# Second self-attention: both head parities in one item, and later keys zeroed after the exponential instead of masked before it

## The reference, cut to what matters

```python
x_norm = x * rsqrt(mean(x*x) + 1e-5) * w_norm
qkv = bit_linear(x_norm, w_qkv)          # 32 query heads, 8 key/value heads, 8 wide
q, k = apply_rotary(q, cos, sin), apply_rotary(k, cos, sin)
scores = einsum('bkgsd,bktd->bkgst', q, k) / sqrt(8)
scores = where(tril, scores, -inf)
attn = softmax(scores, axis=-1)          # 256 queries by 256 keys, causal
out = einsum('bkgst,bktd->bkgsd', attn, v)
return bit_linear(out, w_out)
```

## Time and profile before

| | us |
|---|---|
| median of 3 runs | 3753.85 (3726.41 to 3762.97) |
| the profiled execution's own time | 3760.45 |
| span of the profiled execution | 3758.7 |
| busy over the span: PE, DVE, ACT, POOL | 3073.0, 1924.6, 1550.5, 1177.8 |
| first memset of the stage's token part (POOL) | starts at 2034.49 |
| last DVE instruction of the stage | starts at 2724.14, lasts 0.88 |

### The profile page before, as it was taken

How to read it: one execution, slowest core, us unless ns; L and a number is a source line. 1 busy time by engine, 2 the same in 40 slices (tenths; PEclk the granted TensorE clock), 3 DMA queues, 4 the chain that set the end, 5 groups by cost and what they waited for, 6 DMA issues and landing times. The chain is left out here.

```text
span 3758.7 us, 50944 instructions
## 1 busy us (share of the span) xinstructions
PE 3073.0 (82%) x13981; PEld 1795.9 (48%) x13983; DVE 1924.6 (51%) x4543; ACT 1550.5 (41%) x3160; POOL 1177.8 (31%) x1058
## 2 busy tenths in 40 slices
PE   5799999879999768788794799999957742888884
PEld 2477777557777534444353333333234411355553
DVE  5666666756666567777614455554232340223323
ACT  3555555545555347777511233332225410023331
POOL 1477777367777400000001000000010027044443
PEclk8899999989999855555597589887759965699997
DMA  1122121021111073000000000000000024077885
GB/s 57 46 53 52 35 50 19 12 79 35 51 51 35 23 231 107 1 1 0 27 0 16 0 1 1 1 0 0 1 20 1 0 85 145 9 161 163 182 178 122
DMA packets 127085, 192.73 MB, mean 51 GB/s; under 512 B 17552, under 2 KB 88208, under 8 KB 125584
## 3 DMA queue, kind: packets, MB, share of 16 engines
q1 hardware_dynamic: 83696, 134.71, 12.7%
q0 software_dynamic: 23616, 33.24, 5.0%
q10 hardware_dynamic: 19584, 22.57, 2.2%
HBM read 123.23 MB, written 67.25 MB: 51 GB/s over the span
## 5 line engine op out<-in xcount | busy, mean ns | idle before, releaser
L228 DVE SCALAR_TENSOR_TENSOR h_pre<-h_px,h_par,h_pre 128x510 f32<-128x510 f32 (+2 forms) x384 | 286.5, 746 | 271.3 <-ACT h_pre L689 251.4
L843 POOL TENSOR_TENSOR norm_rstd<-norm_mv,mhalf 128x4 f32<-128x4 f32 x24 | 28.2, 1177 | 1134.9 <-DVE norm_mv L826 1134.9
L652 PE MATMUL h_po<-h_wo,h_h 128*128 128x256 f32 x1024 | 329.9, 413 | 0.0
L2921 POOL DMA_INDIRECT moe_sums<-ex_y,ex_sidx x132 | 204.8, 1552 | 321.0 <-DVE ex_y L3089 304.1
L574 POOL TENSOR_SCALAR h_decay<-h_cumb,h_sel 128x256 f32<-128x256 f32 x256 | 291.6, 1139 | 25.3 <-DMA h_cumb<-cum_rows 25.3
L585 POOL TENSOR_TENSOR h_mix<-h_decay,cb 128x768 f32<-128x768 f32 x128 | 232.9, 1819 | 167.1 <-ACT h_decay L675 167.1
L616 PE MATMUL h_px<-x_cols,h_w 128*128 128x512 f32 x512 | 254.4, 620 | 25.4 <-DMA h_d<-d_skip 25.4
L2038 DVE TENSOR_REDUCE at_nmax<-at_pd 128x2 f32<-128x512 f32 (+1 forms) x192 | 132.5, 690 | 258.9 <-PE at_pd L1772 256.7
L621 PE MATMUL h_pz<-x_cols,h_w 128*128 128x512 f32 x512 | 241.7, 594 | 6.3 <-DVE h_gate L742 6.3
L1256 ACT ACTIVATE xq_ex<-xq_ps,xq_nmax,xq_qs 128x512 f32<-128x512 f32 x256 | 199.4, 779 | 113.6 <-DVE xq_nmax L1324 113.2
L1921 ACT ACTIVATE at_ex<-at_ps 128x512 f32<-128x512 f32 x192 | 114.5, 597 | 291.3 <-PE at_ps L1798 159.7
(11 more groups left out here) (397 smaller groups left out, 6498.6 us busy)
## 6 DMA issues: line engine op xcount, KB each, us to landing
h_cumb<-cum_rows SPq DMA_DIRECT2D x32, 1024.0 KB, 8.4
moe_tiles<-blank SPq DMA_DIRECT2D x4, 6642.0 KB, 44.1
ex_w<-moe_w SPq DMA_DIRECT2D x64, 352.0 KB
ex_xg<-moe_tiles ACTq DMA_DIRECT2D x136, 162.0 KB
ex_wd<-moe_wd SPq DMA_DIRECT2D x64, 176.0 KB
h_w<-w_xg SPq DMA_DIRECT2D x8, 1024.0 KB, 10.4
moe_sums<-blank SPq DMA_DIRECT2D x2, 2176.0 KB, 26.7
h_wo<-w_out SPq DMA_DIRECT2D x8, 512.0 KB, 10.3
```

The source lines that it names most:

```text
L228: ins = dve.scalar_tensor_tensor(out=out[:, :, back:S], in0=src[:, :, 0:S - back], scalar=par[:, at + CK - 1 - back:at + CK - back], in1=o ...
L652: pe.matmul(po[t // TPB][:, t % TPB, :], hh[j % 2][:, t * P:(t + 1) * P], w_out[s.pg][:, j, :], start=(j == 0 and t % TPB == 0), stop=(j = ...
L2921: pool.indirect_dma_start(out=r.sums[i % 2][:, :], out_offset=bass.IndirectOffsetOnAxis(ap=sidx[i][:, 0:1], axis=0), in_=y[i % 2][:], in_o ...
```

## The change

- **Items.** An item is now both head parities: 12 items per batch instead of 24. `at_pd` and `at_ps` become one tile of two banks each (one parity per bank), so `top` reduces 1,024 columns and `exp` takes 1,024.
- **Order of matmuls.** `score` issues even and odd head alternately (partitions 0 to 47, then 64 to 111), then one mask matmul per bank (L1774) for all its heads. `tscore` does the same with 64 rows.
- **Mask.** `tscore` has no mask matmul. Instead POOL sets the exponentials of later keys to zero in place (`select`, L1709, two per item) and `mix` waits for that (`cut`).
- **Mix.** `mix` runs once per group: four matmuls of 512 columns into four strips of 32 partitions, then four of 256. `at_po` is one bank instead of two, and ACT makes the copy (`mcopy`).
- **Elsewhere.** The values are written by ACT (`value`), `splits` and `maxsplit` take both token tiles at once, `qturn` is four pieces in four slots, key and value tiles have three buffers, and two small DVE scalings fold into others.
- **Order of slots.** Every step has a place counted from the batch's first slot (`due`), with 24 slots to a turn. `score` stands on even slots and `tscore` on odd ones; turns are all written out, eleven of them.

```diff
--- before.py
+++ after.py
-        dve.tensor_scalar(amax, amax, BIT_EPS, None, ALU.max)
+        dve.tensor_scalar(amax, amax, BIT_EPS, 1.0 / 127, ALU.max, ALU.mult)
...
-        ex = [sb(f"ex{i}", [P, 512]) for i in range(4)]
+        ex = [sb(f"ex{i}", [P, GD, 2, 512]) for i in range(2)]
...
-        pd = psum("pd", [P, 512])
-        ps = [psum(f"ps{i}", [P, 512]) for i in range(2)]
-        po = [psum(f"po{i}", [P, 2, S]) for i in range(2)]
+        pd = psum("pd", [P, 2, 512])
+        ps = psum("ps", [P, 2, 512])
+        po = psum("po", [P, 2, S])
...
+        SLOTS = 24
+        SQUARE, VAR, XN, QUANT, ITURN, PROJECT, ROTATE, VALUE = 0, 0, 2, (4, 6), 7, 8, (9, 10, 12), 11
+        SPLIT, TURNS = (14, 18), (17, 19, 19, 20, 21, 22)
+        SCORE, MSPLIT, QTURNS, TSCORE = 24, 47, (49, 50, 51, 52), 55
+        MIX, MTURN, DIVIDE = 62, 63, 64
+        OQUANT, OTURN, OUT, ADD = (84, 85), 87, 88, 90
...
+            def select(s, d):
+                n, j = divmod(d, GD)
+                pool.wait_ge(expd, s * ND + d + 1)
+                for par in range(2):
+                    own = ex[n % 2][:, j, par, :].rearrange("p (i t) -> p i t", t=S if j < 2 else P)[:, :, 0:P]
+                    ins = pool.affine_select(out=own, in_=own, compare_op=ALU.is_ge, fill=0.0, base=0,
+                                             pattern=[[0, own.shape[1]], [1, P]], channel_multiplier=-1)
+                ins.then_inc(cut, 1)
...
-                for i, h in enumerate(heads):
-                    lo = 64 * (h % 2)
-                    pe.matmul(pd[:, i * keys:(i + 1) * keys], qT[s.par][lo:lo + PD, h // 2, u * P:(u + 1) * P],
-                              kT[s.par][lo:lo + PD, h // AG, 0:keys], start=True, stop=False)
-                    mm = pe.matmul(pd[:, (i + 1) * keys - P:(i + 1) * keys], r.identb[:], causal[:],
-                                   start=False, stop=True)
+                for i in range(ni):
+                    for par in range(2):
+                        h, lo = head + 2 * i + par, 64 * par
+                        pe.matmul(pd[:, par, i * keys:(i + 1) * keys], qT[s % 2][lo:lo + PD, h // 2, u * P:(u + 1) * P],
+                                  kT[s % 3][lo:lo + PD, h // AG, 0:keys], start=(i == 0), stop=False, skip_group_check=True)
+                for par in range(2):
+                    view = pd[:, par, :].rearrange("p (i k) -> p i k", k=keys)
+                    mm = pe.matmul(view[:, :, keys - P:keys], r.identb[:], causal[:, None, :].to_broadcast([P, ni, P]),
+                                   start=False, stop=True, skip_group_check=True)
...
+            def mix(s, n):
+                pe.wait_ge(cut, s * ND + (n + 1) * GD)
+                pe.wait_ge(valued, s + 1)
+                after(pe, mcopied, s * NGRP + n)
+                for j in range(2):
+                    for par in range(2):
+                        at = VW * (j * 2 + par)
+                        pe.matmul(po[at:at + VW, :, :], val[s % 3][:, 0, 2 * n + j, :], ex[n % 2][:, j, par, :].rearrange("p (i t) -> p i t", i=2),
+                                  start=True, stop=False, skip_group_check=True)
+                for j in range(2):
+                    for par in range(2):
+                        at = VW * (j * 2 + par)
+                        mm = pe.matmul(po[at:at + VW, :, P:S], val[s % 3][:, 1, 2 * n + j, :],
+                                       ex[n % 2][:, 2, par, j * S:(j + 1) * S].rearrange("p (i t) -> p i t", i=2),
+                                       start=False, stop=True, skip_group_check=True)
```

More of the change, by code:

```diff
@@ L1552, in bit_quant, with after @@
     return dve.tensor_scalar(xi, x, ROUND, None, ALU.subtract)
[L1555 to L1567, removed]
+def after(eng, sem, count):
+    if count > 0:
+        eng.wait_ge(sem, count)
 def attn1_tokens(nc, a, r, wqkv, wout, wscale):
@@ L1651, in attn1_tokens @@
         expd = sem("expd")
+        cut = sem("cut")
         mixed = sem("mixed")
@@ L1877, in _ @@
-            first = Batch(0, 0)
-            iturn(first)
-            project(first)
-            for n in range(NB):
-                pturn(first, n)
-            deep_turns(pe, body)
-            oturn(Batch(B - 1, 1))
-            out(Batch(B - 1, 1))
+            for turn, m in slots():
+                for d in range(ND):
+                    if (s := due(turn, m, SCORE + 2 * d)) is not None:
+                        score(s, d)
+                    if (s := due(turn, m, TSCORE + 2 * d)) is not None:
+                        tscore(s, d)
+                for n in range(NGRP):
+                    if (s := due(turn, m, MIX + 2 * GD * n)) is not None:
+                        mix(s, n)
+                    if (s := due(turn, m, MTURN + 2 * GD * n)) is not None:
+                        mturn(s, n)
+                for n in range(NQ):
+                    if (s := due(turn, m, QTURNS[n])) is not None:
+                        qturn(s, n)
+                if (s := due(turn, m, ITURN)) is not None:
+                    iturn(s)
+                if (s := due(turn, m, PROJECT)) is not None:
+                    project(s)
+                if (s := due(turn, m, OTURN)) is not None:
+                    oturn(s)
+                if (s := due(turn, m, OUT)) is not None:
+                    out(s)
+                for n in range(NB):
+                    if (s := due(turn, m, TURNS[n])) is not None:
+                        pturn(s, n)
@@ L2120, in _ @@
[L2120 to L2132 removed]
+            for turn, m in slots():
+                for d in range(ND):
+                    if (s := due(turn, m, SCORE + 2 * d)) is not None:
+                        top(s, d)
+                if (s := due(turn, m, MSPLIT)) is not None:
+                    maxsplit(s)
+                for n in range(NGRP):
+                    if (s := due(turn, m, DIVIDE + 2 * GD * n)) is not None:
+                        divide(s, n)
+                if (s := due(turn, m, VAR)) is not None:
+                    variance(s)
+                if (s := due(turn, m, XN)) is not None:
+                    norm(s)
+                for part in range(2):
+                    if (s := due(turn, m, QUANT[part])) is not None:
+                        quantise(s, part)
+                for part in range(3):
+                    if (s := due(turn, m, ROTATE[part])) is not None:
+                        rotate(s, part)
+                for part in range(2):
+                    if (s := due(turn, m, SPLIT[part])) is not None:
+                        splits(s, part)
+                    if (s := due(turn, m, OQUANT[part])) is not None:
+                        oquantise(s, part)
+                if (s := due(turn, m, ADD)) is not None:
+                    add(s)
```

427 lines of the change are left out of this document (171 added, 256 removed).

## The result

The changed kernel takes 3549.59 us (median of 4 runs, 3545.12 to 3552.57) against 3757.23 us of the kernel before (4 runs, 3726.41 to 3762.97): a ratio of 0.9462, 95% interval 0.9409 to 0.9516. The forecast was 3560 in a range of 3485 to 3635. The profiled run took 3545.12 us, with a span of 3543.3, so 215.3 us less than the profiled run before. The second self-attention went from 690.5 us (2034.5 to 2725.0) to 472.1 us (2030.1 to 2502.2), 218.4 less; what comes ahead of it got 4.4 shorter and what follows it 7.4 longer. The profiled execution of the kernel before was one of its longer ones (3760.45, where its runs begin at 3726.41), so the gain is best taken from the medians, 207.6 us; the 218.4 belong to these two executions.

What follows compares the result with a forecast made beforehand. PE bounds the kernel before; after the change rings and no full engine. Turn 0 at 42, six turns of 53, then 40, 41 and 22 sum to 463 us against 656, giving 3560 us, range 3485 to 3635.

Steps and rivals of the forecast that it cites:

- The forecast case: Second self-attention from turn 0 to its end: 463 us against 656, whole kernel 3560 us; chance 0.48.
- rings: Steady turn: score waits for the last top in one buffer; twelve slot pairs sum to 47 us full clock, 56 half.
- The clock: PE's granted clock in steady turns: a mixture of full and half, between 0.6 and 0.9, giving 51.5 us.
- The rival with the clock risen: PE at full clock, everything overlaps: turns of 44, stage 392 us, total 3490; chance 0.21.
- Strips: PE's parity pairs and the mix's four strips each cost one matmul; mix of a group 1.5 us.
- Prices: Single operations: top 1.25 us, exp 1.02, selects 0.5 and 0.9, a tile 0 score item 1.0.
- Collisions: Selects and DVE standing in each other's way: 1.5 us added to a steady turn.
- the rival's 9 us a turn: GpSimd in the way: selects of 34 us a turn delay DVE about 9 us; turns of 62, total 3625; chance 0.13.
- Steady turns: Full turns of the second self-attention, six counted: 53 us each instead of 75.2.
- heavy pairs: Slot pairs with long DVE work (17.8 us per four, full clock) or a mix with its turn and transposes (18.1).
- the ends: Turn 0 at 42 us, turn 7 at 40, then 41 and 22 us of the tscore-exp ring and last outputs.
- A change of rows costs 0.1 us: PE's score: each change between 48 and 128 rows leaves a weight load unhidden, about 0.1 us.

Runs made afterwards that it cites:

- t_half_top: Changed kernel with DVE's maximum taken over only the first half of each block of scores: 3411.36 us, ratio 0.9326 to before, turn 47.1 us.
- g_late_waits: Changed kernel with iturn, project and the split turns mostly a slot later and the output's add one earlier: 3441.75 us, ratio 0.9398, turn 48.0 us.
- h_mask_late: Changed kernel with tscore mask matmuls instead of selects, and PE's long-wait steps moved: 3407.37 us, ratio 0.9309 to before, stage 409.3 us.
- c_no_select: Changed kernel without the selects and nothing in their place, so later keys are not zeroed: 3531.56 us, ratio 0.9445 to before, turn 54.4 us.
- a_group_masks: Kernel before, with an item's query-key matmuls together in score, then one mask matmul for all heads: 3658.65 us, ratio 0.9788, turn 65.7 us.
- n_group_mix: Kernel before with grouped score masks and the mix of a group's six items in one four-strip burst: 3570.66 us, ratio 0.9771, stage 575.2 us.
- k_fill: Changed kernel with six unneeded matmuls ahead of each of four long PE waits a batch: 3448.56 us, ratio 0.9420 to before, turn 50.8 us.
- f_strip_major: Changed kernel with each strip's 256-column mix matmul right behind its 512-column one: 3537.99 us, ratio 0.9473 to before, stage 472.8 us.

## Why the prediction was right, point by point

The forecast case came: 463 us forecast from the start of turn 0, 438.7 measured (2063.5 to 2502.2), in the place of 655.9. So the stage was forecast 24 us too long, and 3560 is yet only 10 us above the median. Luck has a part in this: the rest of the program got 3 us longer, and the profiled run, forecast at 3567 and measured at 3545.12, stood 4.5 us below its median, where the one before stood above. Within the 24 us, too, errors of both signs met, as the points on turns and ends below show.

- **PE stops being the bound; rings are.** Right. PE is busy 68% of a turn, not the "about 85%" that I wrote, since its work at the mixed clock is 37 us and not the 44 that 85% would be. The sum had it nearly right: 30 us at full and 48 at half the clock make 39 in the middle, which is 74% of 53. t_half_top shows the ring of `score` and `top`, and g_late_waits the long waits.
- **The clock.** "Between 0.6 and 0.9": 0.75. The rival with the clock risen did not come by itself, but h_mask_late has its turn, 44.3 us against the 44 given, at a clock of 0.89.
- **Strips.** One matmul's duration for a pair and for four: right, 4 ns between a pair's starts and 6 to 7 ns between those of a mix. The Trainium skill, TensorEngine Tiling (Array Packing), Key Properties, says that different tiles load and multiply in parallel; the trace agrees, with 1.93 us for four strips of 512 columns against 1.92 for one.
- **Prices.** `top` 1.22 (forecast 1.25), `exp` 1.03 (1.02), eight query-key matmuls and two masks 0.33 + 2 x 0.22 = 0.77 at the full clock (1.0). The 1.0 counts all eight one after another, 8 x 0.06, although a pair was to cost one; 0.1 + 4 x 0.06 + 0.42 = 0.76 follows from the prediction's own rule for a pair. Selects were cheaper than taken: medians 0.41 and 0.63 us (0.5 and 0.9), 12.6 us of POOL a turn instead of 15.
- **Collisions.** I had 1.5 us a turn; DVE's busy time grows by 2.1, of which the turn shows 0.6 (c_no_select). The Trainium skill, SBUF — State Buffer, Who interferes with whom, says that a VectorE instruction with two SBUF inputs and a GpSimd instruction that reads SBUF contend, and that the one that comes second is blocked until the first is done. The trace agrees that each holds the other up: 0.49 us grows to 0.69 beside a select and two selects from 0.77 to 1.05. From when to when one was blocked the rows do not tell. It decides nothing here, since DVE has slack and the rival's 9 us a turn needed selects of 34 us.
- **Steady turns**: 53 forecast, 55.0 measured. I had long waits in the heavy pairs, but not the 4.5 us for the residual add and the 3.0 and 2.8 us at the input's rounding and the split, which g_late_waits took away.
- **Mis-sized: turn 1.** I counted it among six full turns at 53; it took 37.1, since no output of a batch before is finished in it and only nine of the twelve items of `tscore` and two of the four mixes stand in it. That is 16 of the 24 us by which 463 was too long.
- **Mis-sized: the ends.** Turn 0 took 36.1 (42), and from 2413 to the end 89.3 (103). Five turns of 55 instead of 53 stand against it.
- **The step that was not seen: the worth of `tscore`'s mask.** I priced the selects at nothing beyond the collisions and a wait at the end. The sum came out well, but the change would have been 29 us better with the mask left on PE, at 12.3 us for the selects themselves and 16.7 for the clock.
- **"A change of rows costs 0.1 us"** held, and is worth more than the text made of it: a_group_masks got 78 us from that alone.

What stays open: why the clock is granted as it is. It is 0.65 with PE busy 236 of 270 us (n_group_mix), 0.91 with 147 of 203 (k_fill), and 0.94 with 235 of 263 (a_group_masks). So the busy time of PE alone does not tell it, and no run here isolates what does. Nor do the runs separate, in the 144 us of the medians, the merged parities from the new order, the mix and the smaller edits: n_group_mix shows only that the mix alone gains little while other work stands around it.

## What to carry to other kernels

When short matmuls of fewer rows alternate with full ones, group them by shape before anything else: it took one edit and gave two fifths of this gain. When PE is no longer full, moving its last small jobs to another engine may lose time, here 29 us; ask what the clock does, and take out PE's long waits first (32.7 us here for a few moved steps). Add idle matmuls only where long waits remain: they gave 20.2 us in one kernel and cost 16.2 in the next.

## What was unexpected in the hardware

- Order of issue does not bind tiles: with a matmul in between that starts only 1.7 us later, each next strip started 13 ns behind the one before it (f_strip_major).
- Four strips of a float32 mix take as long as one (1.93 us for four of 512 columns, 1.92 for one, at half the clock).
- Work taken from PE can be returned by a lower granted clock (0.94 to 0.65 in n_group_mix, a turn of 67.5 us instead of 65.7), and work added to it can shorten the whole (55.0 to 50.8 us in k_fill).
- A select on GpSimd costs 0.29 us for 128 columns (bfloat16), and in float32 0.41 for 256 and 0.63 for 512: about 0.9 ns a column, where its two-scalar operation takes 3.3.
